# ScalarE's order in layer 1: copies of maxima and raw queries and keys first, squares written in head order

## The reference

```
q_c = x_h W_DQ' W_UQ'            k_c = x_h W_DKV' W_UKV[:16]'     v_c likewise
q_n = q_c * rsqrt(mean(q_c^2) + eps) * q_norm_w      (over the 16 columns of a head)
k_n = k_c * rsqrt(mean(k_c^2) + eps) * k_norm_w
scores = concat(q_n, q_n W_QR') . concat(k_n, x_h W_KR') / 4, causal
out = softmax(scores) v_c W_O'
```

## Time and profile before

| | us |
|---|---|
| timed runs (3): median, lowest, highest | 1711.63, 1711.25, 1713.56 |
| profiled execution: time, span | 1704.8, 1702.8 |
| busy in the span: PE, DVE, ACT, POOL | 1584.4, 1213.1, 1016.8, 470.8 |
| fronts of layer 1 | from 1006 to about 1395 |
| heads' scores in layer 1 (first and last) | 1052.3, 1434.9 |
| sum of squares, 32 in all | 34.4 |
| squares, 32 in all | 20.8 |

### The profile page before, as it was taken

The page is one execution under the profiler, slowest core; times in us unless marked ns, Lnnn a source line. Parts: engine busy times, 40 slices in busy tenths (PEclk is TensorE's granted clock), DMA queues, the critical chain, the costliest instruction groups (busy, mean ns, idle before and its releaser), DMA issues. The chain is left out here.

```text
span 1702.8 us, 29270 instructions
## 1 busy us (share of the span) xinstructions
PE 1584.4 (93%) x9060; PEld 1102.6 (65%) x9060; DVE 1213.1 (71%) x4130; ACT 1016.8 (60%) x2544; POOL 470.8 (28%) x853
## 2 busy tenths in 40 slices
PE   7999999999999999987799977899999998899996
PEld 5667676767676766753588845666666655376765
DVE  4888878887888878755655546999999886134445
ACT  3876767676766767634444454677777766634340
POOL 4001001010101010100275467677786643100001
PEclk9999999999999999998899977999999999999998
DMA  5111111111121211103055628677686665000000
GB/s 165 38 48 45 40 38 38 50 44 48 40 50 38 52 43 38 38 7 100 12 170 163 140 68 113 88 111 106 103 118 87 95 86 98 1 7 25 13 25 31
DMA packets 72583, 111.67 MB, mean 66 GB/s; under 512 B 13265, under 2 KB 38321, under 8 KB 72305
## 3 DMA queue, kind: packets, MB, share of 16 engines
q1 hardware_dynamic: 61024, 81.04, 24.3%
q0 software_dynamic: 10016, 26.48, 6.9%
q10 hardware_dynamic: 1392, 2.29, 0.4%
HBM read 40.04 MB, written 18.87 MB: 35 GB/s over the span
## 5 line engine op out<-in xcount | busy, mean ns | idle before, releaser
L394 ACT ACTIVATE c_probs<-c_probs,a_negmax 128x128 f32<-128x128 f32 (+3 forms) x512 | 280.5, 553 | 0.0
L399 ACT ACTIVATE c_probs<-a_ps_trans 128x512 f32<-128x512 f32 (+1 forms) x256 | 125.0, 488 | 213.0 <-PE a_ps_trans L300 212.1
L1885 ACT ACTIVATE c_probs<-a_ps_st 128x384 f32<-128x384 f32 (+1 forms) x384 | 191.1, 529 | 90.2 <-PE a_ps_st L1685 88.7
L2038 DVE CUSTOM_DVE_ANT_0 a_junk<-a_ps_score,c_mask 128x128 f32<-128x128 f32 (+3 forms) x512 | 220.1, 487 | 33.5 <-PE a_ps_score L1663 30.4
L472 DVE CUSTOM_DVE_ANT_0 c_probs<-a_ps_score,c_mask 128x128 f32<-128x128 f32 (+3 forms) x512 | 219.6, 486 | 15.2 <-PE a_ps_score L281 14.1
L300 PE MATMUL a_ps_trans<-c_ident,c_probs 128*128 128x128 f32 x1280 | 188.0, 277 | 17.6 <-DVE c_probs L489 15.9
L300 PEld LDWEIGHTS a_ps_trans<-c_ident,c_probs 128*128 128x128 f32 x1280 | 146.4, 141 | 87.9 <-issue 39.3
L575 POOL TENSOR_SCALAR a_rstd<-a_mv 128x4 f32<-128x4 f32 x8 | 1.8, 231 | 689.3 <-DVE a_mv L502 689.3
L280 PE MATMUL a_ps_score<-a_kh,a_qs 128*128 128x128 f32 (+3 forms) x512 | 167.2, 350 | 1.3 <-issue 1.1
L489 DVE TENSOR_SCALAR c_probs<-c_probs,a_recip 128x128 f32<-128x128 f32 (+3 forms) x512 | 164.4, 386 | 4.5
L1685 PE MATMUL a_ps_st<-a_qs,a_ks 128*128 128x512 f32 (+3 forms) x512 | 149.7, 362 | 16.7 <-ACT c_probs L1885 8.6
(11 more groups left out here) (290 smaller groups left out, 3157.2 us busy)
## 6 DMA issues: line engine op xcount, KB each, us to landing
a_qs<-a_qlow SPq DMA_DIRECT2D x128, 128.0 KB, 2.2
slot_out<-m_y SPq DMA_DIRECT2D x80, 128.0 KB, 2.0
a_qs<-a_words_even SPq DMA_DIRECT2D x64, 128.0 KB, 4.1
a_ks<-a_words_even SPq DMA_DIRECT2D x64, 128.0 KB, 5.5
c_X<-in_x SPq DMA_DIRECT2D x8, 512.0 KB, 3.9
token_rows<-c_X SPq DMA_DIRECT2D x8, 512.0 KB, 5.7
a_qs<-a_counts SPq DMA_DIRECT2D x32, 128.0 KB, 4.3
a_qs<-a_hid SPq DMA_DIRECT2D x32, 128.0 KB, 4.7
```

The lines of the kernel that those rows point to most:

```text
L394: act.activation(at, at, ACT.Exp, scale=-1.0, bias=negmax[:, n % 4, i:i + 1], accum_out=rowsum[:, n % 4, i:i + 1]).then_inc(s_exp, 1)
L399: act.activation(probT[:, n % 4, TGCOL[grp]:TGCOL[grp] + TGLEN[grp]], ps_trans[(3 * n + grp) % 2][:, 0:TGLEN[grp]], ACT.Copy).then_inc(s_p ...
L1885: act.activation(probT[:, r8, col:col + width], ps_st[item % 2][:, 0:width], ACT.Exp).then_inc(s_stc, 1)
L2038: dve.tensor_tensor_reduce(out=junk[:, to:to + keys], in0=ps_score[g][:, at:at + keys], in1=C.mask[:, L - keys:L], scale=-1.0, scalar=3.0e ...
```

## The change

On ACT, in every slot, `keep_max` and the two `keep` come first, ahead of `high`, `weigh`, `keep_values` and `features`. And `square` now reads `raw` in the order of heads (every fourth word) and writes its result contiguously, `(n h d)`, so that `means` on DVE reads contiguous words.

```diff
-                    act.activation(sq[:, a, :], raw(f, a)[:], ACT.Square, scale=(2 * HD) ** -0.5).then_inc(s_sq, 1)
+                    act.activation(sq[:, a, :].rearrange("p (n h d) -> p n h d", d=HD, h=QUAD),
+                                   raw(f, a)[:].rearrange("p (n d h) -> p n h d", d=HD, h=QUAD),
+                                   ACT.Square, scale=(2 * HD) ** -0.5).then_inc(s_sq, 1)
...
+                    if turned(n) is not None:
+                        keep_max(turned(n))
+                    if front_at(n, 2) is not None:
+                        keep(front_at(n, 2), 0)
+                    if front_at(n, 3) is not None:
+                        keep(front_at(n, 3), 1)
                     if front_at(n, 10) is not None:
                         high(front_at(n, 10), 0)
...
                     if front_at(n, 14) is not None:
                         high(front_at(n, 14), 1)
-                    if front_at(n, 2) is not None:
-                        keep(front_at(n, 2), 0)
-                    if front_at(n, 3) is not None:
-                        keep(front_at(n, 3), 1)
                     if front_at(n, 0) is not None:
                         features(front_at(n, 0))
-                    if turned(n) is not None:
-                        keep_max(turned(n))
...
-                    dve.tensor_reduce(ms[:, a, :, :].rearrange("p t (g h) -> p (t g) h", h=QUAD),
-                                      sq[:, a, :].rearrange("p (n d h) -> p n h d", d=HD, h=QUAD), AX.X, ALU.add
+                    dve.tensor_reduce(ms[:, a, :, :].rearrange("p t h -> p (t h)"),
+                                      sq[:, a, :].rearrange("p (n d) -> p n d", d=HD), AX.X, ALU.add
                                       ).then_inc(s_ms, 1)
```

## The result

The changed kernel took 1716.89 us (median of 22 runs, 1713.82 to 1725.1) and the kernel before, run beside it, 1713.55 (22 runs, 1710.04 to 1718.41). The ratio is 1.0023, with a 95% interval of 1.0015 to 1.0032: 3.9 us slower. The forecast was 1.8 us slower.

The account below looks back on a forecast made before the run. PE was taken to lead, DVE following with slack. With d = 0.39 the terms 1.05 + 0.14 + 0.2 + 0.63 - 0.2 gave +1.8 us on 1711.6: 1713.4 us, range 1710 to 1716, or 1707.3 to 1717.6 reaching into A and B.

Parts of the forecast that it names:

- d: Time added to each ACT square by reading every fourth word: taken as +0.39 us, bounds 0 and +0.65.
- The reduction (1): DVE's `means` reads contiguously: 0.39 us less each, 12.5 us of work in all, worth 0 to 0.8 us.
- The squares (2): ACT's `square`, 652 ns before, reads every fourth word: +0.39 us each, from DVE's price; near 1.04 us.
- the prediction's line: Change in time over layer 1's fronts 4 to 15: -3.8 us plus 1.4 us per 0.1 us of d.
- `keep` before `high` (3): PE's keys' projection starts 0.55 us earlier; in even fronts the third exponential moves by -0.18 + d.
- The sum for the order: With d = 0 the reordering gives -3.8 us, all in fronts 4 to 15, with 0 in the prologue.
- The maxima (4): `keep_max` first starts 0.04 us behind its transpose: 0.16 us gained where `weigh` came first, 0.05 where `features` did.
- The second d in even fronts: In the slot after, ACT's 0.43 us idle takes up the second d; PE leaves slot 61 0.16 us earlier.
- POOL: Its run ends as what PE waits for in even fronts 8, 10, 12: +0.21 or -0.18 us each.
- A: ACT's strided read is free, d = 0, so the reordering gives -3.8 us, 1707.8 us; chance 0.22.
- B: ACT bounds the odd fronts at slots 67 and 68, d 0.5 or more, over 0.2% slower; chance 0.25.
- C: DVE's 12.5 us relief holds the gain, up to 0.8 us at start: some 1711 us; no chance of its own.

Follow-up runs that it names:

- Order with relief: Kernel before, with the new ACT order and contiguous reductions (summing other elements), squares unchanged: -3.6 us, ratio 0.9979.
- the relief alone: Kernel before in the old order, only the reduction made contiguous (summing other elements), squares unchanged: -0.2 us, ratio 0.9999.
- order only: Kernel before with only `keep_max` and `keep` moved first on ACT, squares and reductions unchanged: -0.9 us, ratio 0.9995.
- `keep` first alone: Kernel before with only the `keep` copies moved first, `keep_max`, squares and reductions left as before: -0.3 us, ratio 0.9998.
- keys-only kernel: New order and two Newton steps with sign set right, plus only the keys' squares and sums in head order: -6.2 us against before, ratio 0.9964.
- Two steps in place of three: Kernel before in the old order, POOL's inverse root cut from three Newton steps to two: -4.5 us, ratio 0.9974.
- stride of 2 words: The changed kernel with squares reading every second word instead of every fourth (other elements summed): -4.8 us against before, ratio 0.9972.

## Why the prediction was right, and where it was not

The mechanism and the sign held: the slower squares outweigh what the order gives. Order with relief and the change differ in nothing but the squares, and lie 7.5 us apart (-3.6 and +3.9). What was off is the size of d, and, behind a sum that came out right, the place where the order gives something.

- **The reduction (1).** Predicted 0.39 us a piece and nothing on the path. Measured 0.395, and -0.2 us (-2.1 to +1.9) for the relief alone. Right, in the old order. With the new one it may be worth 2.7 us.
- **The squares (2).** The step that failed in size: the sum's term d was taken from DVE's price, 0.39. ACT paid 0.50 and 0.52. Of its two bounds, 0 and 0.65, it is nearer the upper one. With 0.51 the prediction's line gives +3.5 us, and +3.9 was measured; 1.7 of the 2.1 us that were missing are this term. The rule that spoke against the change (the Trainium skill, Advanced Engine Details and Errata, SBUF Cachelines) held for ACT as well, and more closely than the prediction used it: with two words in each line of 16 bytes the square pays 0.05 us, with one it pays 0.51. In the ten fronts the change took 5.8 us more than order with relief; the prediction's 14.3 us for each us of d, for ten of its twelve fronts, gives 6.1.
- **`keep` before `high` (3).** PE's 0.55 us stall at the projection went in all fronts. The third exponential moved by -0.18 in the order only and by +0.31 with d (step: +0.33), and by +0.49 where `write` stands in the slot (step: d). Right.
- **The sum for the order.** -3.8 us with d = 0: measured -3.6 with the relief, but -0.9 without it. The number agrees with the first and the place does not. The sum had all of it in fronts 4 to 15 and 0 in the prologue. In the traces the ten fronts are no shorter in the new order (248.5 us alone, 247.8 with the relief, 247.4 before), and the start-up is 4.1 and 4.9 us shorter, at a higher clock. As far as single traces can tell, the agreement is luck. In the ten fronts the order gives back later what it takes from PE's stalls, in the slots behind (10.6 to 11.1 us instead of 9.87 or 10.37, in six of the ten fronts alone and in five with the relief).
- **The maxima (4).** The copy was to start 0.04 us behind the transpose. In the change it does so 12 times in 20; 8 times, in slots where `weigh` stood ahead, it starts 0.45 to 0.78 behind, and before it was 0.20 there. PE's own wait for it fell all the same, from 2.2 us to 0.5. In the time it is too small to be told from none: order only is 0.6 us below `keep` first alone, within both intervals.
- **The second d in even fronts.** The sum said that ACT's idle time takes it up. In the keys-only kernel it does in every even front. In the change it does in two of five, and in three the exponential comes 0.6 to 0.7 us later still.
- **POOL.** Two steps in place of three gave 4.5 us in the old order. The sum counted POOL's end in three fronts, and PE stood for it in six of ten; but with those waits gone the ten fronts are no shorter, and 3.6 us come in the start-up, which the sum left out.
- **Rivals.** A (d = 0) fell with the duration, but its time, 3.8 us faster, lies in the interval of the stride of 2 words, where d is 0.05 (-4.8, from -6.5 to -3.3). B (d of 0.5 and more) is what came, at its lower edge. It is there at its place, the exponential behind `write`, but the even fronts, whose idle time stood against it, lost 2.5 of the 6.2 us. C: above.

What stays open: what makes ACT and PE late by some 0.6 to 1.0 us in many fronts of the new order; why the clock of the start-up is higher in the kernels with the new order and cheap squares; and whether DVE's or POOL's relief lets the order's gain through at all. By the line 0.4 us of the measured +3.9 are left, less than the measurement tells.

## What to carry to other kernels

A permutation costs the engine that carries it out, and moving it from one engine to another moves the cost: here 0.39 us on VectorE, which waits for TensorE anyway, became 0.51 us on ScalarE, which TensorE waits for. Before such a move, ask in which slot the engine has idle time (the keys' squares had it), and whether the operand can be read in another way: with two neighbouring words together, or from PSUM before it is copied.

A stall that is seen and removed is worth only what the next one leaves: 5.3 us of waits at one matmul gave 0.9 us, which can't be told from nothing. And a stage's start-up deserves its own sum: by the traces it holds up to 5 us of the differences here, and it had been put at 0.

## What was not expected of the hardware

- ScalarE, 128x512 fp32: 0.65 to 0.68 us contiguous in SBUF, 0.70 to 0.74 with a read stride of 2 words, 1.16 to 1.20 with one of 4 words, 1.12 to 1.14 with a write stride of 16 words. From PSUM with a read stride of 4 words 0.60, no more than contiguous (`keep`, 0.60).
- Profiled executions of one kernel and another differ by up to 10 us ahead of the changed stage (layer 1's first transpose at 1006.6 us in before, 1012.8 to 1017.1 in the others).
- The same matmuls at the start of layer 1 kept PE busy for 31 us at a mean granted clock of 0.74 and for 24 at 0.91.
